# A grouped convolution with an int8 dense layer on one core: the front in a new order, levels of tiles 0 to 27 rounded by VectorE alone

## What is computed

```python
out = conv(x, weight, groups=4, pad=4) + ctx[:, :, None] + bias[None, :, None]
xq  = fake_quant(out, bits=8, axis=-1)       # scale = max|row| / 127
kq  = fake_quant(kernel, bits=8, axis=0)     # scale per column
y   = xq @ kq + fake_quant(ffn_bias, bits=16, axis=-1)
return x + fake_quant(y, bits=8, axis=-1)
```

## Time and profile before

| | |
|---|---|
| median of 3 runs | 283.77 us (283.61 to 284.38) |
| the profiled execution | 282.26 us |
| its span in the trace | 280.5 us |
| DVE, ACT, POOL busy | 76%, 66%, 69% of the span |
| mean granted clock of PE | 0.976 |

### The profile page before, as it was taken

How to read it: one execution, slowest core, us unless ns; L and a number is a source line. 1 busy time by engine, 2 the same in 40 slices (tenths; PEclk the granted TensorE clock), 3 DMA queues, 4 the chain that set the end, 5 groups by cost and what they waited for, 6 DMA issues and landing times.

```text
span 280.5 us, 4237 instructions
## 1 busy us (share of the span) xinstructions
PE 253.2 (90%) x1372; PEld 165.0 (59%) x1372; DVE 211.9 (76%) x447; ACT 185.0 (66%) x278; POOL 194.2 (69%) x104
## 2 busy tenths in 40 slices
PE   7966869999999999999899999799999999999800
PEld 3555557666666666666566566566666666665300
DVE  2598974668777778777978677967778888777674
ACT  4257686446777767667986567867777777755662
POOL 3533332544888888879897788997888888845973
PEclk9979999999999999999999999999999999999975
DMA  6999323530566665646677645565666664444424
GB/s 230 407 411 355 103 92 141 167 137 0 196 220 199 222 211 201 195 167 198 226 272 256 188 155 198 211 239 213 227 225 225 221 232 152 150 151 152 151 116 183
DMA packets 15800, 56.05 MB, mean 200 GB/s; under 512 B 1954, under 2 KB 1954, under 8 KB 15778
## 3 DMA queue, kind: packets, MB, share of 16 engines
q1 hardware_dynamic: 15488, 55.71, 56.2%
q10 hardware_dynamic: 290, 0.07, 0.1%
HBM read 38.99 MB, written 16.78 MB: 199 GB/s over the span
## 4 chain that ended last, share of the span: by engine, by line
POOL 49%; issue 41%; DVE 3%; DMA 3%; ACT 1%; SPq 0%; POOLq 0%; DVEq 0%; PE 0%
POOL x_lo L233 26%; POOL y L241 15%; POOL o_sb L249 8%; DMA k_raw<-ffn_kernel 3%; DVE k_max L558 1%; ACT kq L305 1%; DVE o_sb L665 1%; DVE y_max L656 0%; ACT x_hi L291 0%; SPq L175 0%; DVE k_int L569 0%; DVE dense_ps L590 0%; ACT y_int L349 0%; DVE y L599 0%; DVE last_max L673 0%
## 5 line engine op out<-in xcount | busy, mean ns | idle before, releaser
L456 PE MATMUL dense_ps<-kq,a_t 128*128 128x512 bf16 x496 | 116.7, 379 | 0.0
L233 POOL TENSOR_TENSOR x_lo<-xwin,x_hi 128x1032 fp32r<-128x1032 f32 x32 | 76.6, 2393 | 51.6 <-ACT x_hi L291 51.6
L249 POOL TENSOR_TENSOR o_sb<-y,o_sb 128x1024 f32<-128x1024 f32 x31 | 73.9, 2386 | 24.6 <-ACT y L341 24.6
L456 PEld LDWEIGHTS dense_ps<-kq,a_t 128*128 128x128 bf16 x496 | 47.6, 101 | 45.1 <-issue 0.3
L604 DVE TENSOR_REDUCE small_ps<-conv_ps 128x8 f32<-128x1024 f32 x32 | 39.4, 1232 | 39.6 <-PE conv_ps L422 39.5
L321 ACT CAST a_t<-turn_ps 128x1024 bf16<-128x1024 int16 x32 | 32.4, 1012 | 48.7 <-PE turn_ps L442 48.7
L338 ACT ACTIVATE y_int<-y,y_inv 128x1024 int16<-128x1024 f32 x31 | 35.6, 1147 | 24.1 <-DVE y_inv L647 24.1
L241 POOL TENSOR_TENSOR y<-y,bq 128x512 f32<-128x512 f32 x33 | 41.8, 1273 | 1.0 <-DVE y L590 1.0
L656 DVE TENSOR_REDUCE y_max<-y 128x1 f32<-128x1024 f32 x31 | 37.5, 1211 | 2.3 <-POOL y L241 2.0
L330 ACT ACTIVATE a_int<-conv_ps,inv 128x128 int16<-128x128 f32 x128 | 36.1, 363 | 1.9 <-DVE inv L625 1.9
L291 ACT CAST x_hi<-xwin 128x1032 fp32r<-128x1032 f32 x32 | 33.8, 1055 | 5.3 <-DMA xwin<-x_windows 5.3
(11 more groups left out here) (62 smaller groups left out, 209.1 us busy)
## 6 DMA issues: line engine op xcount, KB each, us to landing
xwin<-x_windows SPq DMA_DIRECT2D x32, 516.0 KB, 4.7
o_sb<-x_rows SPq DMA_DIRECT2D x32, 512.0 KB, 4.5
out<-o_sb SPq DMA_DIRECT2D x31, 512.0 KB, 2.9
k_raw<-ffn_kernel SPq DMA_DIRECT2D x4, 1024.0 KB, 11.9
w_raw<-taps SPq DMA_DIRECT2D x2, 256.0 KB, 3.0
b_row<-ffn_bias SPq DMA_DIRECT2D x1, 512.0 KB, 15.1
out<-o_sb SPq DMA_DIRECT2D x2, 256.0 KB, 2.7
condt<-cond_t ACTq DMA_DIRECT2D x1, 32.0 KB
```

The costliest lines, as they stand in the source:

```text
L233: pool.tensor_tensor(x_lo[:, at].rearrange("p n b -> p (n b)"), xwin[:, t % XWIN, :], x_hi[:, at].bitcast(F32).rearrange("p n b -> p (n b) ...
L249: pool.tensor_tensor(o_sb[:, at, :], y[:, t % YRING, :], o_sb[:, at, :], ALU.add).then_inc(s["o_made"], 1)
L456: mm = pe.matmul(dense_bank(t, h), a_t[:, t % LEVELS, q].rearrange("b j o -> b (j o)"), kq[:, q, half(h)], start=(q == 0), stop=(q == Q - 1))
```

## The change

1. The levels of tiles 0 to 27 (`WHOLE = 28`) are rounded by VectorE alone, 1024 columns in one instruction; ScalarE's `round_levels` returns at once for them. Tiles 28 to 31 stay shared. The waits on `a_rounded` follow.
2. The bias row is loaded as one row, as the first DMA on ScalarE's queue. TensorE spreads it over the partitions with two fp32 matmuls into `dense_ps`, after the first warm-up and ahead of the ctx product. `bias_scale` becomes VectorE's first work behind the masks, ahead of the casts of ctx, and `bias_levels` follows x_hi(0) on ScalarE.
3. ScalarE rounds the blocks 0, 1, 5, 7, VectorE 2, 3, 4, 6. The first scale is spread into the bank of `turn_ps`, and the order of the users is new. Each k_scale is made one column at a time.
4. `conv` is cut in `conv_start` (ctx and x_hi by w_hi) and `conv_rest`. Front orders for TensorE, ScalarE and VectorE are written out up to step 4.
5. GpSimd's `split(1)`, `split(3)` and `split(4)` wait for 2, 3 and 4 blocks rounded by VectorE.
6. Window 2 is loaded ahead of the last pair of blocks.

```diff
-ACT_K = (1, 3)
-DVE_K = (0, 2, 4, 5, 6, 7)
+ACT_K = (0, 1, 5, 7)
+DVE_K = (2, 3, 4, 6)
+WHOLE = 28
...
-        b_row = sb("b_row", [P, F], F32)
+        b_row = sb("b_row", [1, F], F32)
...
+        turn_f32 = turn_ps[:].rearrange("b j p -> b (j p)").bitcast(F32)
+        bias_ps = dense_ps[:].rearrange("p h f -> p (h f)")
...
         def k_bank(user):
-            return dense_ps[:, user % 2 if user < 5 else 1, :]
-
-        K_USERS = (0, 1, 2, 3, "scale0", 4, 5, 6, 7, "scale1")
+            if user == 2:
+                return turn_f32
+            return dense_ps[:, 0 if user in (0, 3) else 1, :]
+
+        K_USERS = (0, 1, "scale0", 2, 3, 4, 5, 6, 7, "scale1")
...
             load_k(2)
+            load_xwin(2)
             load_k(3)
-            load_xwin(2)
-            sp.dma_start(b_row[:], bias.partition_broadcast(P)).then_inc(s["b_in"], 16)
             load_xwin(3)
...
             def split(t):
                 wait(pool, "hi_made", t + 1)
+                wait(pool, "k_rounded_dve", {1: 2, 3: 3, 4: 4}.get(t, 0))
                 wait(pool, "conv_made", t - XSPLIT + 1)
...
         def _(act):
+            act.dma_start(b_row[:], bias.unsqueeze(0)).then_inc(s["b_in"], 16)
             act.dma_start(condt[:], cond_t).then_inc(s["cond_in"], 16)
...
             def round_levels(t):
                 at = t % 2
+                if t < WHOLE:
+                    return
...
             round_x(0)
+            bias_levels()
+            k_round(0)
             k_round(1)
-            k_take(0)
-            k_take(1)
             round_x(1)
-            for k in range(second_step(LAST) + 2):
...
+            for user in range(5):
+                k_take(user)
+            round_x(2)
+            take_levels(0)
+            round_x(3)
+            take_levels(1)
+            round_x(4)
+            k_round(5)
+            k_take(5)
+            round_levels(2)
+            take_levels(2)
+            k_take(6)
+            round_x(5)
+            k_round(7)
+            round_levels(3)
+            k_take(7)
+            k_take(8)
+            take_levels(3)
+            k_take(9)
+            round_x(6)
+            round_levels(4)
+            for k in range(5, second_step(LAST) + 2):
...
+                for t in outs(k)[:1]:
                     quantise(t)
                 if there(k):
                     round_levels(k)
+                for t in outs(k)[1:]:
+                    quantise(t)
...
             pe.wait_ge(s["ident_made"], 1)
             warm_up()
+            pe.wait_ge(s["b_in"], 16)
+            for h in range(2):
+                pe.matmul(dense_ps[:, h, :], ones[0:1, :], b_row[:, half(h)], start=True, stop=True
+                          ).then_inc(s["b_spread"], 1)
             pe.wait_ge(s["cond_made"], 1)
...
+            def conv_start(t):
+                at, g, n0 = t % 2, t % GROUPS, t // GROUPS * NS
+                wait(pe, "a_rounded_dve", t - 1)
+                wait(pe, "a_rounded", t - 1 - WHOLE)
+                wait(pe, "hi_made", t + 1)
...
+                terms(t, ((x_hi, w_hi),))
+
+            def conv_rest(t):
+                terms(t, ((x_hi, w_lo), (x_lo, w_hi))).then_inc(s["conv_made"], 1)
...
                 if t == 0:
-                    pe.wait_ge(s["k_taken"], k_taken_of(f"scale{h}"))
+                    pe.wait_ge(s["k_taken"], len(K_USERS) * (h + 1) // 2)
...
             def k_turn(user):
-                wait(pe, "k_taken", user if user > 5 else user - 1)
+                wait(pe, "k_taken", user if user >= 5 else (0, 0, 0, 1, 2)[user])
+                if user == 0:
+                    pe.wait_ge(s["b_rounded"], 1)
...
+            conv(0)
+            k_turns(0, 2)
+            conv_start(1)
+            k_turns(3, 4)
+            spread_max(0)
+            conv_rest(1)
+            turn_levels(0)
+            conv_start(2)
+            spread_max(1)
+            conv_rest(2)
+            turn_levels(1)
+            dense(0, 0)
+            conv_start(3)
+            spread_max(2)
+            conv_rest(3)
+            k_turn(5)
+            turn_levels(2)
+            dense(1, 0)
+            k_turn(6)
+            conv_start(4)
+            spread_max(3)
+            conv_rest(4)
+            k_turns(7, 8)
+            turn_levels(3)
+            k_turn(9)
+            dense(2, 0)
+            spread_max(4)
+            dense(0, 1)
+            for k in range(5, TILES):
...
-                dve.tensor_scalar(k_scale[:, fs], k_max[:, fs], 1.0 / 127, TINY, ALU.mult,
-                                  ALU.max).then_inc(s["k_scale_made"], 1)
-                dve.wait_ge(s["k_scale_made"], pair + 1)
+                for fb in (2 * pair, 2 * pair + 1):
+                    dve.tensor_scalar(k_scale[:, fb:fb + 1], k_max[:, fb:fb + 1], 1.0 / 127, TINY,
+                                      ALU.mult, ALU.max).then_inc(s["k_scale_made"], 1)
+                dve.wait_ge(s["k_scale_made"], 2 * pair + 2)
...
-                half_n = NS // 2
-                dve.tensor_tensor(a_int[:, at, 0:HALF].rearrange("p (n b) -> p n b", b=BLOCKS),
-                                  conv_cols(at)[:, 0:half_n, :],
-                                  inv8[:, at, 0:half_n].unsqueeze(2)
-                                  .to_broadcast([P, half_n, BLOCKS]), ALU.mult
+                mine = NS if t < WHOLE else NS // 2
+                dve.tensor_tensor(a_int[:, at, 0:mine * BLOCKS]
+                                  .rearrange("p (n b) -> p n b", b=BLOCKS),
+                                  conv_cols(at)[:, 0:mine, :],
+                                  inv8[:, at, 0:mine].unsqueeze(2)
+                                  .to_broadcast([P, mine, BLOCKS]), ALU.mult
...
             k_levels(0)
-            for k in range(TILES):
+            k_levels(1)
+            column_max(0)
+            levels(0)
+            column_max(1)
+            levels(1)
+            column_max(2)
+            scale_half(0, 0)
+            k_levels(2)
+            levels(2)
+            add_bias(0, 0)
+            column_max(3)
+            scale_half(1, 0)
+            k_levels(3)
+            levels(3)
+            add_bias(1, 0)
+            for k in range(4, TILES):
```

More of the change, by code:

```diff
@@ L402, in _, with terms @@
             warm_up()
-            def conv(t):
-                at, g, n0 = t % 2, t % GROUPS, t // GROUPS * NS
-                x_at = t % XSPLIT
-                wait(pe, "a_rounded_dve", t - 1)
-                wait(pe, "a_rounded", t - 1)
-                wait(pe, "hi_made", t + 1)
-                for hs in range(2):
-                    ns = slice(n0 + hs * NH, n0 + (hs + 1) * NH)
-                    mm = pe.matmul(
-                        conv_ps[:, at, hs, :].rearrange("p (n b) -> p n b", n=NH),
-                        ctx2[:, g].rearrange("k q o -> k (q o)"),
-                        select[:, ns].unsqueeze(2).to_broadcast([P, NH, BLOCKS]),
-                        start=True, stop=False, skip_group_check=True)
-                for x, w in ((x_hi, w_hi), (x_hi, w_lo), (x_lo, w_hi)):
+            def terms(t, pairs):
+                at, g, x_at = t % 2, t % GROUPS, t % XSPLIT
+                for x, w in pairs:
                     if x is x_lo:
                         wait(pe, "lo_made", t + 1)
+                    if t == 0 and w is w_lo:
+                        pe.wait_ge(s["w_lo_made"], 2)
                     for ch in range(2):
@@ L426, in conv @@
                                 start=False, stop=False, skip_group_check=True)
-                mm.then_inc(s["conv_made"], 1)
+                return mm
+            def conv_start(t):
[3 more added lines that the diff above has]
+                wait(pe, "hi_made", t + 1)
+                for hs in range(2):
+                    ns = slice(n0 + hs * NH, n0 + (hs + 1) * NH)
+                    pe.matmul(
+                        conv_ps[:, at, hs, :].rearrange("p (n b) -> p n b", n=NH),
+                        ctx2[:, g].rearrange("k q o -> k (q o)"),
+                        select[:, ns].unsqueeze(2).to_broadcast([P, NH, BLOCKS]),
+                        start=True, stop=False, skip_group_check=True)
+                terms(t, ((x_hi, w_hi),))
+            def conv_rest(t):
+                terms(t, ((x_hi, w_lo), (x_lo, w_hi))).then_inc(s["conv_made"], 1)
+            def conv(t):
+                conv_start(t)
+                conv_rest(t)
             def spread_max(t):
@@ L490, in k_turns @@
                     k_turn(user)
[L492 removed]
+            conv(0)
[27 more added lines that the diff above has]
+            for k in range(5, TILES):
                 again = seconds(k)
[L494 to L495 removed]
                 conv(k)
[L497 to L521 removed]
+                turn_levels(k - 1)
+                if len(again) == 2:
+                    dense(again[0], 1)
+                dense(k - LAG, 0)
+                spread_max(k)
+                dense(again[-1], 1)
             dense(LAST - 1, 0)
@@ L683, in _ @@
             k_levels(0)
```

(15 more changed lines are left out.)

85 lines of the change are left out of this document (20 added, 65 removed).

## The result

| | before | after |
|---|---|---|
| median of 7 runs each | 283.77 us (281.34 to 284.67) | 288.06 us (285.73 to 290.68) |
| ratio, 95% interval | | 1.0143 (1.0086 to 1.02) |
| the profiled execution | 282.26 us | 288.39 us |
| its span | 280.5 us | 286.7 us |
| mean granted clock of PE | 0.976 | 0.942 |

The kernel became slower by 1.4%, 4.3 us in the medians and 6.1 us in the profiled executions. The ratio leaves out the slowest run after (290.68 us, over 1.5% above the quickest) and so compares 287.85 with 283.77 us. Of the 39 executions of the kernel before beside the experiments eleven took 280.6 to 282.3 us, with a mean granted clock of 0.975 to 0.980, and the others 282.9 to 285.1 us, with 0.962 to 0.969.

What follows compares the result with a forecast made beforehand. PE's work and waits were taken to bound the middle. Profiled: 282.26 + 2.65 (front) + 2.4 (clock) - 2.4 (levels) = 284.9 us; the same change of 2.65 on the median gives 286.4, range 281.9 to 288.0.

Steps and rivals of the forecast that it cites:

- Levels by VectorE alone: Middle, two double steps: rounding grows to 1.22 us, PE's 1.41 us waits go, saving 2.4 us (bounds 0 and 2.8).
- ScalarE in the front: Four activations fewer per tile, 1.12 us, were said to give nothing in a middle step, where ScalarE isn't the bound.
- rival (2): Whole kernel faster, 282.8 or 282 us: cheap bias matmuls, clock holds, both catch-up waits go in full; chance 0.20.
- The start: Up to k_levels(0): bias row matmuls take 3.4 us, 0.85 of it reaching VectorE's chain, moving k_levels(0) from 10.60 to 11.45.
- Conv(0), which nobody waits for: Front: PE's second warm-up and conv(0) move by 3.4 us to about 16.4, without anyone waiting for them.
- The waits: Front, x_lo of tiles 3 and 4: 8.8 us chains make PE wait 4.6 and some 4.2 us; conv(5) at 55.9.
- The clock: Behind both new waits: two falls, each a low stretch of 3.3 us, costing 2.4 us together (bounds 0 and 3.3).
- (1): Front: the clock holds through both new waits, giving 284.0 us; chance 0.20.
- (3): Double steps: the longer rounding delays VectorE, so PE's wait only moves to the spread; no saving, 288.8 us; chance 0.08.
- (4): Middle steps: rounding from PSUM takes over 2.0 us and VectorE becomes the bound, 289 us and more; chance 0.07.

Runs made afterwards that it cites:

- experiment 3: The changed kernel, but VectorE alone rounds only the levels of tiles 0 and 1, ScalarE sharing from tile 2 on: 289.30 us, ratio 1.0228.
- experiment 4: The kernel before, with ScalarE's half of the levels put between the two quantisations of a two-output step: 280.97 us, ratio 0.9881.
- experiment 2: The kernel before with its old front, levels of tiles 0 to 27 rounded by VectorE alone: 276.92 us, ratio 0.9783.
- experiment 6: The changed kernel with unused fp32 matmuls filling PE's waits before the x_lo matmuls of tiles 3 and 4: 284.60 us with two, 283.07 with four.
- experiment 7: The changed kernel with k_levels(2) and k_levels(3) ahead of the half scales on VectorE: 279.63 us, ratio 0.9869.
- experiment 9: The changed kernel, GpSimd's waits one tile later, K levels before half scales, ScalarE reordered, VectorE alone for tiles 0 to 4: 276.23 us; bias load last: 276.44.
- experiment 1: The changed kernel with GpSimd's waits one tile later, split(3) free, split(4) and split(5) waiting: 277.93 us, ratio 0.9829.
- experiment 8: The changed kernel with the bias row as the last of four small loads on ScalarE's queue: 288.14 us, ratio 1.0156.

## Why the prediction was right, and where its sizes were off

The sign and the two causes were right: slower, by two PE waits at x_lo, with 2.4 us won back in the middle. The time came 1.7 us above the forecast in the medians (288.06 for 286.4), at the upper end of the range and above the forecast's own range, 284.8 to 287.5 (its clock bounds of 0 and 3.3 us give 284.0 to 287.3, so neither covers it); on the profiled execution, whose time the sum was made for, it is 3.5 us (288.39 for 284.9). There the forecast loss was 2.65 us and the measured 6.1. That the medians lie nearer is in part luck: the forecast added the change of the profiled execution to the median of before, and most executions of before are slower than the profiled one, at a lower mean clock. And 0.3%, which the prediction took as what a measurement can tell, is too fine here: the runs of one kernel spread over 1.2% (before) and 1.7% (after), so the interval of the ratio is what decides. By steps:

- **Levels by VectorE alone.** Said: rounding 1.22 us, idle 0.8 us, a step of 7.35, both waits gone, the spread 0.2 late, 2.4 us. Measured: 1.22, 0.80, 7.35 (91.26 to 98.61), no wait at the transposes, the spread held up by VectorE (0.52 us for its weight load at 150.23), 2.5 us. Right. The sentence that the order of the second quantisation in ScalarE has no weight was right for this kernel and hid something: experiments 3 and 4 show that the order alone takes the same waits away. The change has two sufficient causes for one gain, and I named one.
- **ScalarE in the front.** That four activations less "give nothing" was said of a middle step, and then not asked for tiles 0 to 4. There they are worth 2.3 us in the old front (experiment 2, profiled executions; 4.4 in the medians) and 2.6 in the new one (experiment 3), clock included. In the sum for the new front the activations were simply left out of ScalarE's list, so that the forecast had this gain without naming it; but rival (2), faster, was judged without it.
- **The start.** k_levels(0) said 11.45, measured 11.33. The parts were off against each other: the bias row's matmuls took 1.98 us, not 3.4, while the small loads behind the new one came 3.5 us later than before (copy of cond at 8.13; 4.61 before). I had costed that load at 0.4 us of issue. The 3.4 wasn't wrong for the kernel: in the profiled executions of experiments 3, 6 (two matmuls) and 7 and the first of 9, with the same order ahead of the ctx product, the row took 3.78 us, PE had no wait for cond and the clock didn't fall there. Conv(0) then ended at about 17 us too (17.03 in experiment 3).
- **"Conv(0), which nobody waits for".** Wrong. It ended at 17.2, and the transposes of the first K blocks, which stand behind it in PE's own list, started there, so that ScalarE took the first at 17.86 and then waited another 0.80 us for PE's next two, behind conv_start(1). With this dense(0,0) came at 28.16 instead of 27.3: 0.9 us. In the second execution of experiment 6 the transposes began 1.63 us earlier (15.57) and dense(0,0) 1.53 us earlier (26.63).
- **The waits.** The chain was said to be 8.8 us with a wait of 4.6; it was 8.66 with 4.22 (28.16 to 36.82). The second: 9.41 with 3.72, said 8.8 with 4.2. The second chain is longer because dense(1,0) itself ran at the low clock (40.42 to 43.10, against 28.16 to 30.09). Right, link by link.
- **The clock.** The term that failed. Said: two falls, each with a low stretch of 3.3 us, 2.4 us together and 3.3 at most. Measured: low stretches of 6.8 and 10.2 us, and 5.0 to 5.5 us (experiment 6). A third fall, at 7.8 us in PE's wait for cond, was not in the forecast. I took the length of a low stretch from the one at the start of before, where PE was then fully busy. Here 1.7 us of the first stretch still lay in the wait (35.1 to 36.82), and the second began only 7 us after the first had ended and held one more wait (1.10 us before 53.89). That this thinner work kept the clock down is argued, not shown; in experiment 7 PE was busy without a gap from 35.62 to 42 us, behind its one wait, and that stretch was 3.4 us. The length also differs between executions with nearly the same work: the early stretch was 3.4 us in before and 6.8 in experiment 2. Without a clock effect the forecast from dense(0,0) to conv(5) was 28.65 us, and experiment 6 measured 28.21. So of the 3.6 us by which conv(5) came later than forecast (61.88 for 55.9 + 2.4) 0.9 are dense(0,0) and 2.7 the clock.

The Trainium skill, TensorE: Matmul & The Clock Gate, section "HAM oscillation — how this bites in real kernels", says that a long enough wait between bursts of matmuls makes the next burst start at half rate. The trace agrees that a fall follows such waits: 4.22, 3.72, and the 2.71 us of experiment 7 were each followed by one, the 0.22 us by none. What the runs add is how long it lasts: 6.8 us for the first, 10.2 for the second, and 3.4 us for the 2.71.

The rivals: (1), the clock holds, was set at 284.0; experiment 6 made that case and gave 283.07 with its waits mostly filled. (2), faster, did not come, but the point from which it decides was the right one: with the waits gone the front is 2.1 us shorter (experiment 1). (3) and (4) did not show: the spread was late by a quarter of a microsecond, and the rounding took 1.22 us.

**Why GpSimd's waits are there at all.** In before the two-column scale of VectorE took 2.32 us, from 17.82 to 20.14, while GpSimd's x_lo ran from 17.74 to 20.12:

```profile
17.74 2.38 POOL L233 TENSOR_TENSOR x_lo<-xwin,x_hi 128x1032 fp32r<-128x1032 f32 x1 [6.18 <-ACT x_hi L291]
```

The Trainium skill, SBUF — State Buffer, under "Who interferes with whom", says that VectorE, in its two-port modes, and GpSimd contend for one shared pair of ports, and that the one who issues second blocks fully. The two rows agree: the short operation began second and ended with the long one. But that collision cost VectorE some 2 us once, while the waits that avoid it for tiles 3 and 4 cost the kernel 10.7 us in the profiled execution. And for tile 3 there was nothing to avoid: in experiment 1 its x_lo ends at 29.12, while VectorE's next small scale operations came at 33.43 and took 0.21 us for two, and its work during x_lo was on PSUM at its usual lengths (1.22 us from 26.79, 1.23 from 28.21).

Left open: why the small loads behind the bias row's land some 3.4 us later (experiment 8 shows that the order on the queue does it, and not how), why the row's matmuls take 1.98 us in some executions and 3.78 in others, how the clock ran in the median executions of before, and whether the load's place matters once the waits are right (experiment 9: 276.23 and 276.44, with runs of 274.4 to 278.5).

## What to carry to other kernels

A wait that is put in to keep two engines apart must be priced at the one who waits for the waiting engine, here PE two links further, and not at the collision that it avoids. A gap of PE costs its own length and can cost most of that again in clock (here 5.0 us behind 7.9 us of waits), so an estimate needs the time until the clock is back, and not one stretch read elsewhere. And when two edits of a change could each remove the same wait, try each alone: here three lines of order did for the middle what a redistribution of work was made for.

## What was not expected of the hardware

- **The clock's way back.** Behind waits of 4.22 and 3.72 us the granted clock stayed at its lower level for 6.8 and 10.2 us, in experiment 3 for 10.2 both times; a fill of 3.6 us of unused matmuls in each wait kept it at the upper one throughout 30 to 62 us, one of 1.88 us let it fall once.
- **One instruction, two durations early on.** The same two fp32 matmuls of 512 columns took 3.44 us as the first warm-up (1.43, four passes) and 1.98 us for the bias row at 4.79 in after, and 3.78 us for the bias row at 5.13 in experiment 7; the fillers at 30.90 took 3.60 us for eight passes. Passes of 0.85 and 0.43 us stand in the clock's ratio of two, while the records show a granted clock of 1.00 for all of them. In the first microseconds the granted clock of the profile thus can't be read as the rate.
- **A fall without a long wait.** In the five profiled executions with the bias row by PE in which the row took 1.98 or 2.10 us the clock fell at 7.8 to 8.8 us, in experiment 8 (at 7.9) with PE at work from 5.75 on. In the four in which it took 3.78 us it stayed up until the waits for x_lo, or throughout the front. No run separates cause and effect here.
- **A 4 KB load ahead of three small ones** on the same queue moved what waits for the last of them from 4.77 to 8.13 us (experiment 8 against after; 7.27 to 8.52 in the other six executions with the load first).
